# Row sums of squares by products with a ones column, a new order of pieces at a stage boundary, and a moved residual step at the end

## The reference, cut to what matters

```
y = _qlora_linear(h, ...)
mu = mean(y); var = mean(square(y - mu))
y = (y - mu) * rsqrt(var + EPS) * g + b
y = gelu(y); y = _qlora_linear(y, ...); h = y + h
```

## Time and profile before

| what | us |
|---|---|
| median of 3 runs | 2295.22 (2295.1 to 2296.44) |
| the profiled execution | 2293.41 |
| its span, first to last instruction | 2291.5 |
| stage 1 with the seam | 0 to about 590 |
| stage 2 | about 592 to 1790 |
| stage 3 | to 2291.5 |
| mean granted TensorE clock | 0.992 |

### The profile page before, as it was taken

The page is one execution under the profiler, slowest core; times in us unless marked ns, Lnnn a source line. Parts: engine busy times, 40 slices in busy tenths (PEclk is TensorE's granted clock), DMA queues, the critical chain, the costliest instruction groups (busy, mean ns, idle before and its releaser), DMA issues.

```text
span 2291.5 us, 35692 instructions
## 1 busy us (share of the span) xinstructions
PE 2231.2 (97%) x11837; PEld 1867.4 (81%) x11837; DVE 1491.0 (65%) x2747; ACT 1281.3 (56%) x2450; POOL 691.4 (30%) x993
## 2 busy tenths in 40 slices
PE   8999999998799999999999999999999899999997
PEld 7999999997678878788788787887878788888886
DVE  4666666676666756756656666666665766766666
ACT  4555555555646445454544544544545677777775
POOL 3565565566100101001001010010100255555555
PEclk9999999999899999999999999999999999999999
DMA  6132221244201102011020020110221313333322
GB/s 167 38 111 82 101 93 62 101 147 125 94 1 56 56 19 74 18 55 55 0 92 18 23 84 2 55 55 18 73 69 55 129 60 106 110 110 110 110 92 74
DMA packets 101704, 166.12 MB, mean 72 GB/s; under 512 B 19664, under 2 KB 22480, under 8 KB 101520
## 3 DMA queue, kind: packets, MB, share of 16 engines
q1 hardware_dynamic: 98960, 164.74, 21.3%
q10 hardware_dynamic: 2688, 0.66, 0.1%
HBM read 115.05 MB, written 50.33 MB: 72 GB/s over the span
## 4 chain that ended last, share of the span: by engine, by line
PE 63%; DVE 5%; ACT 4%; issue 1%; POOL 1%; DMA 0%; POOLq 0%; DVEq 0%
PE quant_bank L1732 7%; PE quant_bank L1734 7%; PE quant_bank L1733 7%; PE quant_bank L2123 6%; PE quant_bank L2124 6%; PE quant_bank L2125 6%; PE quant_bank L1766 4%; PE quant_bank L1768 4%; PE quant_bank L1767 4%; PE quant_bank L1787 2%; PE quant_bank L1789 2%; PE quant_bank L1788 2%; ACT quant_h_hi L1559 1%; PE quant_bank L1718 1%; PE quant_bank L2140 1%; PE quant_bank L1783 1%
## 5 line engine op out<-in xcount | busy, mean ns | idle before, releaser
L1495 POOL TENSOR_TENSOR quant_up_rstd<-quant_up_var,quant_minus_half 128x4 f32<-128x4 f32 x48 | 48.6, 1012 | 888.4 <-DVE quant_up_var L1619 888.4
L1732 PE MATMUL quant_bank<-quant_h_hi,kept_W_hi 128*128 128x512 f32 x768 | 306.2, 399 | 5.2 <-DVE quant_h_lo L1592 5.1
L1734 PE MATMUL quant_bank<-quant_h_lo,kept_W_hi 128*128 128x512 f32 x768 | 304.7, 397 | 0.0
L1733 PE MATMUL quant_bank<-quant_h_hi,kept_W_lo 128*128 128x512 f32 x768 | 303.5, 395 | 0.0
L1536 ACT ACTIVATE quant_sq<-quant_bank,quant_b_root 128x512 f32<-128x512 f32 x192 | 131.9, 688 | 248.3 <-PE quant_bank L1734 247.8
L2088 DVE TENSOR_TENSOR mlp_g_lo<-quant_bank,mlp_g_hi 128x512 fp32r<-128x512 f32 x256 | 176.3, 689 | 106.3 <-ACT quant_bank L2025 106.2
L2024 ACT ACTIVATE mlp_g_hi<-quant_bank,mlp_b 128x512 fp32r<-128x512 f32 x256 | 177.6, 694 | 70.8 <-PE quant_bank L2125 63.5
L1766 PE MATMUL quant_bank<-quant_g_hi,kept_W_hi 128*128 128x512 f32 x512 | 207.8, 406 | 0.0
L1768 PE MATMUL quant_bank<-quant_g_lo,kept_W_hi 128*128 128x512 f32 x512 | 202.5, 396 | 0.0
L1767 PE MATMUL quant_bank<-quant_g_hi,kept_W_lo 128*128 128x512 f32 x512 | 202.4, 395 | 0.0
L1559 ACT ACTIVATE quant_h_hi<-kept_x_in 128x512 fp32r<-128x512 f32 x128 | 80.7, 631 | 208.1 <-DVE kept_x_in L1647 121.4
(11 more groups left out here) (299 smaller groups left out, 5822.6 us busy)
## 6 DMA issues: line engine op xcount, KB each, us to landing
delta_x_in<-L_attn_x_d SPq DMA_DIRECT2D x16, 1024.0 KB, 8.0
delta_x_res<-L_attn_x_d SPq DMA_DIRECT2D x16, 1024.0 KB, 6.0
x_d<-delta_z SPq DMA_DIRECT2D x64, 256.0 KB, 2.1
quant_y<-x_d SPq DMA_DIRECT2D x16, 1024.0 KB, 5.0
x_d<-quant_y SPq DMA_DIRECT2D x16, 1024.0 KB, 4.2
mlp_x_in<-x_d SPq DMA_DIRECT2D x16, 1024.0 KB, 10.4
mlp_x_res<-x_d SPq DMA_DIRECT2D x16, 1024.0 KB, 6.5
out_d<-mlp_z SPq DMA_DIRECT2D x15, 1024.0 KB, 8.9
```

Of the source, the lines that this page charges most:

```text
L1732: mm(tr[j][:, :], W_hi[2 * b][:, k, cols], h_hi[m][:, k, :], start=k == 0, stop=False)
L1733: mm(tr[j][:, :], W_lo[2 * b][:, k, cols], h_hi[m][:, k, :], start=False, stop=False)
L1734: last = mm(tr[j][:, :], W_hi[2 * b][:, k, cols], h_lo[m][:, k, :], start=False, stop=k == KT - 1)
```

## The change

There are three edits.

1. `total` on PE makes four float32 products instead of four transposes: stationary operand is the same 128x128 piece of `sq`, moving operand is one column of ones, and the result is one column of the bank. DVE then copies 128 x 4 values instead of reducing 128 x 512. One memset on POOL fills the column, and the first `total` waits for it.
2. `TAIL` gets a new order. `O` and `ogT` move ahead of `tile.0.2`, the `attn` pieces ahead of most of the layer 1 tiles, and the pieces `la_hi.4/5`, `la_lo.4/5`, `tile.1.2` and `tile.1.3` to the end; `la_lo` of layers 4 and 5 waits for the last `shift` instead of for `ogT_lo`.
3. In the last step of stage 3 POOL does `residual` before `leave` of the step before, and DVE's wait for POOL's scaled rows is made row by row.

```diff
         TAIL = tail("""
-            stats.2' lbT.0 stats.3' lbT.1 U wU tile.0.0 norm.2' norm.3' lbT.2 PT low.0.0 tile.0.1 S new_S.0 new_S.1 low.0.1 tile.0.2 O low.0.2 tile.0.3 lbT.3 low.0.3
-            ogT dequant.3.1 tile.1.0 low.1.0 dequant.3.2 dequant.3.3 attn.0 tile.1.1 la_hi.4 la_lo.4 la_hi.5 la_lo.5 attn.1 z.0 stats.0 low.1.1 tile.1.2 lbT.4 z.1 attn.2 low.1.2 lbT.5
-            stats.1 norm.0 tile.1.3 attn.3 z.2 low.1.3 stats.2 norm.1 z.3 stats.3 norm.2 norm.3""")
+            stats.2' lbT.0 stats.3' lbT.1 U wU tile.0.0 norm.2' norm.3' lbT.2 PT low.0.0 tile.0.1 S new_S.0 new_S.1 O ogT low.0.1 tile.0.2 low.0.2 tile.0.3 lbT.3 low.0.3
+            dequant.3.1 attn.0 attn.1 z.0 stats.0 tile.1.0 low.1.0 attn.2 z.1 stats.1 norm.0 tile.1.1 attn.3 z.2 stats.2 low.1.1 norm.1 lbT.4 z.3 stats.3 la_hi.4
+            norm.2 lbT.5 la_hi.5 dequant.3.2 tile.1.2 norm.3 la_lo.4 la_lo.5 low.1.2 tile.1.3 dequant.3.3 low.1.3""")
...
-                    pool.wait_ge(s_["ogT_lo_done"], GROUPS * CHUNKS)
+                    pool.wait_ge(s_["shift_done"], GB * GROUPS * CHUNKS)
...
+            nc.gpsimd.memset(one_column[:, :], 1.0).then_inc(one_filled, 1)
...
-                nc.vector.tensor_reduce(up_var[m][:, :], by_rows, mybir.AxisListType.X, ALU.add).then_inc(s["up_var_done"], 1)
+                nc.vector.tensor_copy(up_var[m][:, :], shared[:, 0:RT]).then_inc(s["up_var_done"], 1)
...
+                if isinstance(t, int) and (t, m, b) == (0, 0, 0):
+                    pe.wait_ge(one_filled, 1)
                 for r in range(RT):
-                    last = nc.tensor.transpose(by_rows[:, r, :], sq[m][:, 0, r * P:(r + 1) * P], ident)
+                    last = mm(shared[:, r:r + 1], sq[m][:, 0, r * P:(r + 1) * P], one_column[:, :], start=True, stop=True)
                 last.then_inc(s["sum_ps"], 1)
...
         def step(t, i, first, last):
+            if last:
+                residual(t, i)
             if not first:
                 leave(*before(t, i))
-            residual(t, i)
+            if not last:
+                residual(t, i)
...
-            if r == 0:
+            if isinstance(t, int) and u == STEPS - 1:
+                dve.wait_ge(s_["x_done"], n - RT)
+            elif r == 0:
                 wait(dve, s_["x_done"], RT * u)
```

More of the change, by code:

```diff
@@ L1276, in quantised_and_low_rank_steps @@
         minus_half = sb("minus_half", [P, RT])
+        one_column = sb("one_column", [P, 1])
         rstd_row = sb("rstd_row", [P, R])
@@ L1284, in quantised_and_low_rank_steps @@
         S = [{n: sem(f"{n}_{m}") for n in names} for m in range(STREAMS)]
-        filled, b_done = sem("filled"), sem("b_done")
+        filled, b_done, one_filled = sem("filled"), sem("b_done"), sem("one_filled")
         w_ = {n: sem(f"weights_{n}") for n in ("dequant_done", "wT_ps", "w_mean_done", "W_hi_done", "W_lo_done")}
```

## The result

The changed kernel takes 2311.91 us (median of 4 runs, 2311.49 to 2312.29), the kernel before 2295.16 on the same chip (4 runs, 2292.77 to 2296.44). That is a ratio of 1.0077, 95% interval 1.0065 to 1.0089, so slower by 0.65 to 0.89%. The forecast was 2313.4 with a range of 2304 to 2319. The profiled execution took 2311.49 with a span of 2309.7, where the sum gave 2311.6.

A forecast was written before the change was run, and what follows sets the result against it. The prediction took PE, 97% busy and full in stage 2, to bound the kernel. Edits 1, 2 and 3 summed +21.1 - 1.4 - 1.5 = +18.2 us: 2311.6 for the profiled execution, 2313.4 for the median, range 2304 to 2319.

The forecast's parts named there:

- lower bound of 0.055: The 48 `total` groups on PE: shortest distance between record starts, 0.055 us; 8 records at 0.44 us would be no change.
- rival (a): The 48 `total` groups: one-column stream sets the pace or product is one record; edit 1 free, -2.9 us, 2292.3; chance 0.08.
- rival (c): DVE waits and seam: 5.1 us of waits vanish, queue doesn't bind, seam gives 4.7; +9.8 us, 2305; chance 0.06.
- The walk along the list: Seam, new order at today's durations: `attn.0` about 570.3, DVE's last z about 579.2, last scaled rows 4.7 us sooner.
- (b): The `total` groups: only columns count, loads hide under the product before; with edits 2 and 3 -24 us, 2271; chance 0.05.
- (d): The `total` groups: float32 records partly serialise with products around them, another 0.11 us a group, +5 us, 2318.7; chance 0.04.

The follow-up runs named there:

- four-record kernel: Changed kernel with the row sum written as float32r and two float32r columns of ones, four records a group instead of eight; 2291.45 us, ratio 0.9988 to the kernel before.
- fastest kernel: Four-record kernel with the bias and late low-rank loads issued between second and third store of the group before; 2289.96 us, ratio 0.9976 to the kernel before.
- half loads: Changed kernel with 64 instead of 128 columns of `sq` as stationary operand, sums of the other rows left out; 2304.55 us, ratio 1.0041 to the kernel before.

## Why the prediction was right

**Edit 1, +21.1 predicted, +21.5 measured.** The price of a record was right (0.11 taken, 0.112 measured), and so was the number of records. The lower bound of 0.055, which rival (a) leaned on, was the distance within one pair, L1086's; the first two products of a group show such a distance too (0.026 with one column, 0.055 with 64), but only once in a group, and the loads set the rest. The group's 0.44 is 0.449. What remained argument in the prediction, that the load and not the stream sets the pace, was shown by two runs: 64 columns cost the same as one, and four loads in the place of eight bring back the 0.44. The first is also what the 64-column rows of stage 1 had said; they were the right neighbour. The section "LDWEIGHTS (loading the stationary operand)" of the Trainium skill's "TensorE: Matmul & The Clock Gate" holds here with both widths: by its rule a load of 128 and one of 64 columns take 107 and 53 ns, where 0.112 and 0.058 us were measured, and so the trace agrees. Its "Back-to-back issue gap", 25 ns for 1 to 64 columns, does not describe a sequence with a load for each product: the records are 0.112 apart with one column and with 64, but for the first two. The section itself gives that figure for the gap alone and says that in a stream of loads and products both set the spacing, so it is no rule against the load's, as the prediction has it. Its own figure for such a stream is about 81 ns at 128 columns; the transposes here are 0.109 us apart, and the measurement decides.

**DVE, zero predicted, zero measured.** The copy took 0.162 us where 0.2 was taken. The waits stayed at 5.1 us to the last digit, and rival (c)'s gain from them was refuted by the four-record kernel.

**Edit 2, -1.4 predicted, -2.07 in the changed kernel, -1.4 to -2.6 over five kernels with the new order and an unchanged queue.** The mechanism is as told: the last rows are ready 3.4 us sooner, the queue drains at full rate and sets the end. The traces with moved and added loads, and the last store's time to land, show the queue binding in the new order and not in the old one. The size was a little low; one part of that is that the queue carried 0.49 MB behind 586 (247 GB/s for 2 us) and not 0.60. The walk along the list ran ahead of what came: `attn.0` at 571.94, not 570.3 (0.9 of that is the later `U`), DVE's last z at 580.22, not 579.2, and the pieces of the weights' preparation end at 586.2 on DVE and near 586.7 on POOL, not 585. Since the queue bound, this cost nothing; in the fastest kernel, whose queue is dry by then, POOL stands idle for only 2.17 us before stage 2, where it was 3.77 in the changed kernel, so those pieces are about as late as the queue there.

Part of this gain may be given back. PE resumes at a granted clock of 0.50, that is 1.2 GHz, after standing still from 581.25 to 590.54, and from its first record to the first product of block 0 it takes 5.11 us, where it was 4.82 before. This stretch scatters from one execution to the next: 4.82 to 5.68 us in the five traces with the old order (mean 5.25) and 4.95 to 6.40 in the seven with the new one (mean 5.80). That is about 0.5 us against the new order, with ranges that overlap; the 1.5 us either way that the prediction kept for this covers it.

**Edit 3, -1.5 predicted, -1.33 measured,** -1.34 alone. The product, not the add, now releases z, as told. z starts 0.13 behind the product's end (2296.94), where the sum had it start with it.

**Not predicted: the closing, -1.19.** Behind the last `total` DVE waits for a load of the residual in the kernel before, and PE for DVE. The wait in the kernel before, in the changed one:

```profile
1790.55 0.69 DVE L1666 TENSOR_TENSOR quant_y<-quant_bank,quant_y 128x512 f32<-128x512 f32 x1 [3.31 <-DMA quant_y<-x_d]
```
```profile
1809.93 0.69 DVE L1668 TENSOR_TENSOR quant_y<-quant_bank,quant_y 128x512 f32<-128x512 f32 x1 [1.88 <-DMA quant_y<-x_d]
```

The three kernels with eight full loads and no other change there (after, edit 1 alone, 64 columns) take 27.81, 27.98 and 27.92 us from the last `total` to stage 3, the eight others with four records a group 28.78 to 29.13, and the one with half loads 26.16. The load isn't issued any sooner: it goes out 14.30 us behind the start of the last record of `total` before and 14.41 after. It lands faster, in 5.25 us where it took 6.68 (5.34 and 5.40 in the other two with full loads, 5.19 with half loads, 6.20 to 6.70 with four records). So edit 1 costs 21.5 us in the groups, and this transfer gives back about 1 of it. The span of edit 1 alone is even so 21.3 us longer, since that trace is 0.6 longer ahead of the first `total` and 0.2 in stage 1. Why the transfer is faster stays open.

**The sum.** +18.2 was forecast for the spans and +18.19 came, by luck as to the last digit: +0.4 (groups), -0.7 (seam), +0.3 (clock), -1.2 (closing), +0.2 (end) and +0.9 in stage 1 cancel. The change doesn't touch stage 1 up to the last `U`, and that record starts between 558.79 and 562.01 in the twelve traces, so the 0.9 is scatter. The median lies 1.5 below the forecast since the distance from the profiled execution to the median, taken as 1.8 from the kernel before, is 0.4 in the kernel after; both are single executions out of a scatter of that size. Rivals (a) and (b) fail at the load spacing of 0.112, (d) at a group of 1.356, with no extra load's worth in it, (c) at the 5.1 us of waits that stay and at a seam of -2.07 where it wanted -4.7.

## What to carry to other kernels

Count weight loads, not columns, when a product's moving operand is narrow: at one column as at 64 a product here cost what its 128 stationary columns took to load, and plain float32 paid twice. The relief of an engine at 65% was worth only the waits that it removed, here none, while the added work on the engine at 97% came out in full. At a boundary between stages, ask whether the queue or the last computed store sets the end, and read it from that store's time to land. Here a reordering of engine work uncovered the queue, and only then did loads moved into its idle time shorten the seam.

## What the runs showed of the hardware

- Narrower stationary operands between wide ones save less than their loads: eight 64-column loads between 128-column ones run 0.058 us apart, but their group is 0.30 us longer than this gives, with no load started under the product before.
- When a product with 512 columns runs before such a group, the first two one-column products start 0.026 us apart and the next ones 0.112: the shortest distance in a trace isn't the pace.
- Loads of float32 and of float32r pieces had records of 0.19 us and the same distance of 0.11; a float32r product is one record with one load, as a transpose is, and a float32 product two.
- Adding 1 MB to the queue cost 2.33 us in one order of the same work and 0.83 in the other, at the same 0.4 MB/us.
- A store of 256 KB landed 2.02 us after its issue where the queue didn't hold it up, and PE's first record of the next stage came 1.72 to 1.76 us behind the landing in all twelve traces.
